# A graph network on one Trainium2 core: each slot list stored four times in DRAM, and each broadcast load reading the four copies

## The reference, cut to what matters

```
h = x @ W_enc.T + b_enc
for l in range(2):
    m = concatenate([h[row], h[col]], axis=-1)
    m = relu(m @ msg_W1[l].T + msg_b1[l])
    m = m @ msg_W2[l].T + msg_b2[l]
    agg = segment_sum(m, col, num_segments=N)
    upd = concatenate([h, agg], axis=-1) @ upd_W[l].T + upd_b[l]
    h = layer_norm(h + upd, ln_g[l], ln_b[l])
```

## Time and profile before

| | |
|---|---|
| median of 3 runs | 3507.04 us (3503.56 to 3512.03) |
| the profiled execution | 3502.89 us, of which the traced span is 3501.0 us |
| mean granted TensorE clock | 0.931 of full speed |
| busy share: PE, PEld, DVE, ACT, POOL | 85%, 78%, 69%, 59%, 23% |
| DMA, mean over the span | 163 GB/s, 570.13 MB |
| first message layer, first and second pass | about 644 to 964 us, 964 to 1349 us |
| second message layer, first and second pass | about 1455 to 1754 us, 1754 to 2145 us |

### The profile page before, as it was taken

The page is one execution under the profiler, slowest core; times in us unless marked ns, Lnnn a source line. Parts: engine busy times, 40 slices in busy tenths (PEclk is TensorE's granted clock), DMA queues, the critical chain, the costliest instruction groups (busy, mean ns, idle before and its releaser), DMA issues.

```text
span 3501.0 us, 221482 instructions
## 1 busy us (share of the span) xinstructions
PE 2972.4 (85%) x88750; PEld 2729.9 (78%) x88750; DVE 2400.5 (69%) x5707; ACT 2058.7 (59%) x3873; POOL 800.4 (23%) x1161
## 2 busy tenths in 40 slices
PE   3665666699989998799989997789999799999998
PEld 2544544588878887688878887688888799999998
DVE  6899998555545556666645555699999865556555
ACT  1333333577766666777756665667777555555555
POOL 1222215200012225400012124334333411111111
PEclk7777777899999999999999999799999999999999
DMA  3000002699978883599977875055555478877888
GB/s 68 9 7 7 6 6 53 141 214 216 216 180 201 198 201 88 121 219 217 223 180 195 199 197 123 16 164 172 170 170 171 137 219 276 274 243 232 263 269 251
DMA packets 423266, 570.13 MB, mean 163 GB/s; under 512 B 129597, under 2 KB 277877, under 8 KB 423186
## 3 DMA queue, kind: packets, MB, share of 16 engines
q1 hardware_dynamic: 390475, 541.83, 57.2%
q0 software_dynamic: 8000, 16.40, 4.7%
q10 hardware_dynamic: 24710, 10.93, 1.2%
HBM read 459.97 MB, written 108.98 MB: 163 GB/s over the span
## 4 chain that ended last, share of the span: by engine, by line
PE 57%; DVE 16%; issue 9%; DMA 9%; SPq 3%; POOL 2%; ACT 2%; DVEq 1%; POOLq 0%; ACTq 0%
PE psum L1544 16%; PE psum L1315 15%; PE psum L1333 7%; PE psum L1319 7%; DMA tabf<-slots_turned 5%; DVE arena L1583 5%; PE psum L1531 4%; PE psum L1511 2%; PE psum L684 1%; PE psum L1519 1%; POOL arena L2019 1%; DVE Hf L1057 1%; DVE Hf L918 1%; DVE AGGf L963 1%; POOL tabf L2002 1%
## 5 line engine op out<-in xcount | busy, mean ns | idle before, releaser
L1315 PE MATMUL psum<-tabf,arena 125*32 125x128 f16 x40256 | 1112.4, 220 | 105.9 <-issue 58.4
L1315 PEld LDWEIGHTS psum<-tabf,arena 125*32 125x32 f16 x40256 | 949.5, 97 | 197.8 <-issue 129.9
L1319 PE MATMUL psum<-arena 96*32 96x128 f16 x20928 | 1054.3, 221 | 10.4 <-issue 10.4
L1366 ACT ACTIVATE arena<-psum 128x512 f32<-128x512 f32 x1300 | 770.5, 596 | 426.1 <-PE psum L1319 387.7
L1319 PEld LDWEIGHTS psum<-arena 96*32 96x32 f16 x20928 | 693.6, 95 | 19.0 <-issue 9.6
L1544 PE MATMUL psum<-tabr,cellr 125*125 125x256 f32 x5000 | 620.2, 284 | 14.4 <-ACT cellr L1462 14.4
L1544 PEld LDWEIGHTS psum<-tabr,cellr 125*125 125x125 f32 x5000 | 602.8, 187 | 15.8 <-issue 15.8
L1333 PE MATMUL psum<-arena 128*32 128x129 f32 x10400 | 564.1, 278 | 1.7 <-issue 1.7
L1462 ACT CAST cellr<-arena 125x630 fp32r<-125x630 f16 x500 | 359.9, 720 | 270.2 <-PE psum L1544 197.0
L1573 ACT CAST arena<-psum 125x500 f16<-125x500 f32 x625 | 358.9, 578 | 153.0 <-PE psum L1511 109.6
L1401 DVE TENSOR_TENSOR AGGf<-AGGf,psum 125x129 f32 x404 | 116.0, 287 | 435.6 <-PE psum L1333 432.9
(11 more groups left out here) (302 smaller groups left out, 4369.1 us busy)
## 6 DMA issues: line engine op xcount, KB each, us to landing
arena<-cells_kept SPq DMA_DIRECT2D x500, 315.0 KB
cells_kept<-arena SPq DMA_DIRECT2D x625, 126.0 KB
arena<-slots_turned SPq DMA_DIRECT2D x152, 384.0 KB
tabf<-slots_turned SPq DMA_DIRECT2D x150, 384.0 KB
arena<-slots_turned SPq DMA_DIRECT2D x152, 192.0 KB
tabf<-slots_turned SPq DMA_DIRECT2D x150, 192.0 KB
arena<-slots_turned SPq DMA_DIRECT2D x50, 512.0 KB
tabf<-slots_turned SPq DMA_DIRECT2D x50, 512.0 KB
```

The source lines that it names most:

```text
L1315: pe.matmul(psCell[b][q:q + GW, g * D:(g + 1) * D], fr, rows, start=g == 0 and p == 0, stop=False, tile_position=(0, q), skip_group_check= ...
L1319: m = pe.matmul(psCell[b][q:q + GW, g * D:(g + 1) * D], toB[part][:, here + q:here + q + GW], cur[:, part, g, :], start=g == 0 and 4 * k + ...
L1366: act.activation(msgs[:, SLOT[pos], :, 0:D], psCell[SLOT[pos]].rearrange("p (c d) -> p c d", d=D), ACT.Relu).then_inc(f_msg, 1)
```

## The change

`slots_turned` gets a leading dimension of COPIES = 4. `store` writes the same `STb` four times, once into each copy, so ACT issues four DMAs where it issued one, and every count of the semaphore `o_store` is four times as large. `lists` now reads all copies in one DMA: the source's outermost dimension counts the 4 copies, the next one repeats a copy's row 32 times (16 times for a = 1), and the last one is the row. The destination is the same 128 (or 64) partitions as before, so partitions 0 to 31 get their row from copy 0, 32 to 63 from copy 1, and so on. Before, the source had one dimension of 128 (or 64) repeats outside the row. Bytes and number of loads are unchanged.

```diff
+COPIES = 4
...
-        slots_dram = nc.dram_tensor("slots_turned", [NT + 2, 2, KS, RG * CELL], F16, kind="Internal").ap()
+        slots_all = nc.dram_tensor("slots_turned", [COPIES, NT + 2, 2, KS, RG * CELL], F16, kind="Internal").ap()
+        slots_dram = [slots_all[n] for n in range(COPIES)]
...
                 act.wait_ge(o_ST, m + 1)
-                act.dma_start(slots_dram[at].rearrange("o a k (g e) -> (a k g) o e", g=RG), STb[:, v]).then_inc(o_store[v], 16)
+                for copy in slots_dram:
+                    act.dma_start(copy[at].rearrange("o a k (g e) -> (a k g) o e", g=RG), STb[:, v]).then_inc(o_store[v], 16)
...
             for u in range(2):
-                act.wait_ge(o_store[u], 16 * (SORTS // 2 + 1))
+                act.wait_ge(o_store[u], 16 * COPIES * (SORTS // 2 + 1))
...
                 for a, rows in ((0, 128), (1, CP * GW)):
-                    sp.dma_start(slist[w][half][0:rows, a, 0:(k1 - k0) * RG * CELL], slots_dram[at, a, k0:k1, :]
-                                 .rearrange("o k e -> o (k e)").to_broadcast([rows, (k1 - k0) * RG * CELL])).then_inc(f_list[w][half], 16)
+                    width = (k1 - k0) * RG * CELL
+                    sp.dma_start(slist[w][half][0:rows, a, 0:width], slots_all[:, at, a, k0:k1, :]
+                                 .rearrange("n o k e -> n o (k e)").to_broadcast([COPIES, rows // COPIES, width])).then_inc(f_list[w][half], 16)
...
             for u in range(2):
-                sp.wait_ge(o_store[u], 16 * (SORTS // 2 + 1))
+                sp.wait_ge(o_store[u], 16 * COPIES * (SORTS // 2 + 1))
```

More of the change, by code:

```diff
@@ L839, in sort_act @@
                         copy_ranks(i * 4 + (2 * k + u + 6), u)
-                    store(i * 2 + (k + 1), 1 - k, bass.ds(i * 4 + (2 * k + 3), 2), bass.ds(i * 4 + (2 * k + 2), 2), i * 16 + 16)
+                    store(i * 2 + (k + 1), 1 - k, bass.ds(i * 4 + (2 * k + 3), 2), bass.ds(i * 4 + (2 * k + 2), 2), i * (16 * COPIES) + 16 * COPIES)
                     for u in range(2):
@@ L845, in sort_act @@
             m = SORTS - 1
-            store(m - 1, 1, slice(2 * m - 1, 2 * m + 1), slice(2 * m - 2, 2 * m), 16 * (SORTS // 2))
+            store(m - 1, 1, slice(2 * m - 1, 2 * m + 1), slice(2 * m - 2, 2 * m), 16 * COPIES * (SORTS // 2))
             act.wait_ge(s_bound, 1)
@@ L851, in sort_act @@
             normalise(lambda w: slice(2 * m + w, 2 * m + w + 1))
-            store(m, 0, slice(2 * m + 1, 2 * m + 3), slice(2 * m, 2 * m + 2), 16 * (SORTS // 2))
+            store(m, 0, slice(2 * m + 1, 2 * m + 3), slice(2 * m, 2 * m + 2), 16 * COPIES * (SORTS // 2))
             act.wait_ge(s_turned, 1)
@@ L2285, in _ @@
                 pool.sem_inc(empty, 1)
-            pool.sem_inc(o_store[1], 16)
+            pool.sem_inc(o_store[1], 16 * COPIES)
             for stored in l_keep:
```

## The result

The changed kernel takes 4770.6 us (median of 4 runs, 4768 to 4782) against 3505.3 us of the kernel before: 1.362 times as long (95% interval 1.360 to 1.365).

What follows compares the result with a forecast made beforehand. It took list loads on four engines at 20.7 GB/s each to bound all four passes: 3502.9 - 1378 + 3320 + 20 = 5465 us, said as 5460, with a range of 4850 to 6700 us (0.85).

Steps and rivals of the forecast that it cites:

- What bounds the kernel now: Message layers: list loads bind one pass of four, but a list load twice as long would bind every pass.
- what a pass loads: List loads: 1.18 MB per tile in a first pass, 1.38 MB in a second, beside stacked and table rows.
- How many DMA engines: List loads: 4 outermost in the source gives 4 engines instead of 16; chance 0.90.
- The rate of one engine: List loads on four engines: 20.7 GB/s each, 82.8 GB/s together, with 14.1 and 24.2 as ends.
- the sum's terms: Message passes: 15.7 and 17.5 us per tile, 3320 us in place of 1378, plus 20 us at the start.
- the fast end: Four engines at 24.2 GB/s each and no idle time: passes take 2730 us, 4875 us in all.
- Two engines share one way: Rival on the way into the partitions: 15 to 17 GB/s per engine, 6190 to 6730 us; chance 0.25.
- ACT's stores cost 0: Sort: ACT's 75 more issues hide under its waits for PE, cost 0; uncovered 24 us.
- the start costs 20 us: Start of the first layer: the eight first list loads take 28.5 us instead of 9, +20 us.
- SP's list issues, 0: SP's list loads: up to 120 us more issue time, but four issues stand under 15 us of transfer: 0.
- The faster rival: List loads: 16 engines stay and copies remove a crowd at one address; first layer's first pass -10 us, about 3490; chance 0.04.

Runs made afterwards that it cites:

- e2: Kernel before, one copy stored once; list loads read it with an outermost dimension of 4 of step 0; 4762.1 us, 1.3596 of the kernel before.
- e9: Kernel before, one copy; only the 64-partition (a = 1) loads get 16 repeats outermost, then 4 of step 0; 3482.0 us, 0.9941 of the kernel before.
- e1: Changed kernel, four copies still stored, but every list load reads copy 0 in the old shape; 3507.3 us, 1.0013 of the kernel before.
- e3: Changed kernel with 32 (or 16) repeats outermost and the four copies as the dimension inside; 3468.3 us, 0.990 of the kernel before.
- e11: The kernel of e3 (four copies inside, repeats outermost) measured once more; 3482.0 us, 0.9932 of the kernel before.
- e5: The shape of e3 with one copy: all list loads have 32 (or 16) repeats outermost, then 4 of step 0; 3479.3 us, 0.9928 of the kernel before.
- e12: The one-copy kernel of e5 measured once more, beside e11; 3484.5 us, 0.9939 of the kernel before.
- e8: Kernel before, one copy; list loads read it with an outermost dimension of 16 of step 0; 3507.9 us, 1.0010 of the kernel before.

## Why the prediction was right and wrong

- **What bounds the kernel now, what a pass loads:** right. A load that got slower bound all four passes.
- **How many DMA engines:** right, and shown now for two sides that differ: 4 and 8 outermost against 128 or 64 partitions give 4 and 8 engines, by the closing packets (9648 and 6432 fewer) and the share. A dimension of step 0 counts like any other (e2). The Trainium skill's rule (DMA: Bandwidth & Descriptors, on why a DMA increments its semaphore by 16 and not by 1) says so of both access patterns; the traces agree.
- **The rate of one engine:** this step failed. The prediction took "the middle of 19.0 and 22.4, 20.7 GB/s", and a queue busy 0.96 of the time, which is 19.9 GB/s over all. It had named this itself as what to look for: a share near 0.25, and a rate far from 83 GB/s (the windows show 105 to 107). Measured: in the second layer's first pass an engine carries 295 KB of lists and 16.5 KB of other rows in 12.34 us, 25.2 GB/s; in its second pass 348 KB in 13.9 us, 25.0 GB/s, idle time included. With 25.0 the sum's terms are 12.5 and 13.9 us per tile: 3502.9 - 1378 + 2640 + 20 = 4785 us, 0.3% from the measured time. The rate is measured and put in, so this tests only the rest of the sum, which holds. Even the value at the fast end, 24.2 GB/s, was short: in that microsecond the 85 list packets of 4096 bytes took 162 ns each, which is 25.3 GB/s, so the uncrowded rate stood in the trace of before; five packets of 1024 bytes at 115 ns pulled the mean down. What the runs put in place of the step: with the new dimension outermost, a packet of 3072 bytes takes 125 ns at 4 engines, 143 at 8 and 213 at 16. So the rate among sixteen says little of the rate among four, and I should have put the value at the uncrowded end. The number of engines isn't all of it: at 16 engines the shape alone moves a packet between 213 and 172 ns (e9).
- **Two engines share one way:** did not happen. With four engines the packets are the shortest of all, 125 ns.
- **ACT's stores cost 0, the start costs 20 us:** right within what can be told (e1: at most 0.3%; the start: 16 us).
- **SP's list issues, 0:** right in time, but not for the reason given. Issues hold SP for 1.8 us, since the engines behind it are full.
- **The faster rival:** I priced it at 10 us by the second layer's first pass, 5.92 us per tile, as if that were PE's own pace. It was not: e3, e9 and e11 run both first passes at 5.7 us per tile. In the first layer less crowding brings about 20 us, from 6.1 to 5.7 us per tile (e3, e5, e9, e11 and e12). In the second layer what held PE was mostly the pause of 0.2 us, which e5 and e12 keep though their packets are short (170 ns there, from the packet records). So of the 0.6 to 1% that the runs gain, about 20 us are shown to come from the loads; the other 8 to 13 us, where a run has them, come with the pause gone.

Open: why the 64-partition loads crowd the engines in one shape and not in the other, and what makes PE pause in the second layer. e8 shows that it isn't their shape alone: its a = 1 loads have the same 16 by 4 repeats as e9's, but its a = 0 loads are 16 by 8 where e9's are 128, and the packets stay at 213 ns. So it is the pair of shapes that matters. The Trainium skill (SBUF — State Buffer, the DMA port swizzle) says that partitions 0 to 63 reach only the 8 even ports; sixteen engines that write 64 partitions would then have to share ports. That holds for both shapes alike, so it doesn't tell them apart by itself, and no run here measured a port.

## What to carry to other kernels

Read the outermost dimension of both sides of every DMA before anything else: the largest common divisor up to 16 of the two was the number of engines in every list load here, and a dimension of 4 put outermost for a good reason cost 36%. Count closing packets and multiply the DMA share by 16 to see how many engines a load has. A low share beside a waiting consumer meant few engines here, not a light load. When a broadcast crowds, try copies or repeats inside and the large count outside (0.6 to 1% here), and compare with the same shape of step 0 before crediting the copies. Before crediting either, look at the passes one by one: part of the gain may lie where nothing waits for a load.

## What the runs showed that I had not expected

- One engine among four moves 25 GB/s, idle time included, at one address as at four (e2 and the changed kernel, 125 and 126 ns per 3072-byte packet); among sixteen, in the shape of the kernel before, it moved 14.
- The split of the 64-partition loads alone changes the time of the kernel by 0.6% (e9 against before), with the same bytes from the same address.
- With the queues full, the chain names SP's issues (66.5%) and not the DMA, though the four engines are what is full.
- A PE-bound pass has two paces that the loads don't explain: 5.7 us per tile, and 5.95 with a pause of 0.2 us in each (e3 and e5, the second layer's first pass).
